# Last stage of a three-stage kernel: PE's probability transposes move to the front of each step

## What is computed

```python
def _L0_ffn_ref(x, W_gate, W_qkv):           # x = layernorm(h), 16 heads of 32
    gating = softmax(x @ W_gate.T)
    indicator = one_hot(argmax(gating)); gating_top1 = indicator * max(gating)
    q, k, v = split(x @ W_qkv.T)
    k_shared = einsum('bth,bthd->btd', indicator, k)
    v_shared = einsum('bth,bthd->btd', gating_top1, v)
    att = einsum('bhqd,bkd->bhqk', q, k_shared) / sqrt(hd)
    att = softmax(where(causal, att, -inf))
    y = einsum('bhqk,bkd->bhqd', att, v_shared)
h = h + y
```

## Time and profile before

| | us |
|---|---|
| median of 3 runs | 1482.92 |
| lowest, highest | 1481.59, 1484.98 |
| the profiled execution | 1483.9 |
| its span, first to last instruction | 1482.1 |
| PE busy in the span | 1322.8 (89%) |
| DVE, ACT, POOL busy | 816.1, 595.5, 452.5 |

### The profile page before, as it was taken

The page is one execution under the profiler, slowest core; times in us unless marked ns, Lnnn a source line. Parts: engine busy times, 40 slices in busy tenths (PEclk is TensorE's granted clock), DMA queues, the critical chain, the costliest instruction groups (busy, mean ns, idle before and its releaser), DMA issues. The chain is left out here.

```text
span 1482.1 us, 23784 instructions
## 1 busy us (share of the span) xinstructions
PE 1322.8 (89%) x8504; PEld 1109.5 (75%) x8504; DVE 816.1 (55%) x1629; ACT 595.5 (40%) x1777; POOL 452.5 (31%) x696
## 2 busy tenths in 40 slices
PE   0799999999999995599999998489899998999997
PEld 0678888888888884478888886368788787878775
DVE  8656656655566321455555552345666656566566
ACT  3443333333334221333333321234546556454646
POOL 3555445544554310233333231021221203122121
PEclk9999999999999997799999999599999999999999
DMA  3222222222222225856655411354141423514040
GB/s 147 98 87 93 93 105 88 93 93 100 86 93 93 93 90 177 241 164 171 171 162 162 147 43 44 141 107 93 37 100 36 93 70 62 116 40 101 16 93 30
DMA packets 59525, 150.71 MB, mean 102 GB/s; under 512 B 7696, under 2 KB 24336, under 8 KB 57872
## 3 DMA queue, kind: packets, MB, share of 16 engines
q1 hardware_dynamic: 59408, 149.18, 34.0%
HBM read 67.37 MB, written 56.62 MB: 84 GB/s over the span
## 5 line engine op out<-in xcount | busy, mean ns | idle before, releaser
L724 PE MATMUL psum<-wr_high,x_high 128*128 128x512 f32 x576 | 234.1, 406 | 5.0 <-DVE x_low L541 5.0
L724 PE MATMUL psum<-wr_high,x_low 128*128 128x512 f32 x576 | 228.9, 397 | 0.0
L724 PE MATMUL psum<-wr_low,x_high 128*128 128x512 f32 x576 | 228.3, 396 | 0.0
L1466 ACT ACTIVATE probs<-psum,row_max 128x256 f32<-128x256 f32 (+1 forms) x384 | 165.1, 453 | 107.6 <-issue 75.2
L1716 POOL TENSOR_TENSOR picked_rows<-picked_rows 128x768 f32<-128x768 f32 (+1 forms) x64 | 61.0, 953 | 269.6 <-DVE picked_rows L1600 265.8
L724 PEld LDWEIGHTS psum<-wr_high,x_high 128*128 128x128 f32 x576 | 109.0, 189 | 28.6 <-DVE x_low L541 5.8
L724 PEld LDWEIGHTS psum<-wr_high,x_low 128*128 128x128 f32 x576 | 108.7, 189 | 25.9
L1618 DVE TENSOR_REDUCE row_max<-psum 128x2 f32<-128x512 f32 (+1 forms) x160 | 109.5, 684 | 31.8 <-PE psum L1821 31.8
L724 PEld LDWEIGHTS psum<-wr_low,x_high 128*128 128x128 f32 x576 | 109.1, 189 | 23.4
L937 ACT ACTIVATE square_scratch<-psum 128x128 f32<-128x128 f32 x192 | 50.7, 274 | 185.4 <-PE psum L1130 185.4
L698 PE MATMUL psum<-m,basis 128*128 128x64 f32 x384 | 76.8, 283 | 40.8 <-POOL m L650 40.8
(11 more groups left out here) (200 smaller groups left out, 3027.5 us busy)
## 6 DMA issues: line engine op xcount, KB each, us to landing
qk<-stage SPq DMA_DIRECT2D x24, 512.0 KB, 2.6
v<-stage SPq DMA_DIRECT2D x24, 512.0 KB, 2.6
g<-gate_rows SPq DMA_DIRECT2D x24, 512.0 KB, 2.6
q_stack_t<-q_t_high SPq DMA_DIRECT2D x64, 192.0 KB, 4.2
q_stack_t<-q_t_low SPq DMA_DIRECT2D x64, 192.0 KB, 5.8
qk_rows<-qk SPq DMA_DIRECT2D x16, 512.0 KB, 5.5
v_rows<-v SPq DMA_DIRECT2D x16, 512.0 KB, 6.9
gate_rows_q<-g SPq DMA_DIRECT2D x16, 512.0 KB, 8.9
```

What stands on the lines that cost most here:

```text
L724: last = nc.tensor.matmul(psum[:, PB[(6 * u[1] + n) % 4], :], x[:, q, k], ww[:, w, k, :], start=c == 0, stop=c == 3 * KC - 1)
L1466: last = nc.scalar.activation(pr[:, g % 2, c], psum[:, SB[g % 3], c], ACT.Exp, scale=SCALE_F, bias=mx[:, g % 3, 1, x:x + 1], accum_out=dsu ...
```

## The change

The four probability transposes of step g are issued before the scores of step g+2 and before the side piece, instead of behind both. Nothing else differs.

```diff
--- before.py
+++ after.py
@@ -1919,10 +1919,10 @@
 
             def step(i, n, back, ahead):
                 g = NS_F * i + n
+                p_transposes(g)
                 if g + 2 < LAST:
                     scores(g + 2)
                 side(i, n, back, ahead)
-                p_transposes(g)
                 if n == 0 and back:
                     values(i - 1, 11)
                 if n in (1, 2, 3, 4):
```

## The result

| | before | after |
|---|---|---|
| median (runs) | 1482.92 (5) | 1501.17 (5) |
| lowest, highest | 1476.81, 1484.98 | 1500.75, 1502.93 |
| span of the profiled execution | 1482.1 | 1499.0 |
| ratio after/before, 95% interval | | 1.0126 [1.0103, 1.015] |

The change costs 18 us, 1.3%. The sign was forecast, the size wasn't: +7.8 us and a range up to 1499.

The account below looks back on a forecast made before the run. PE itself was taken as the bound in middle pairs, losing only a handful of stalls. About +0.7 us per pair, +4.9 for seven, made +7.8 with the last pair: 1491.7 profiled, 1490.7 median, range 1484 to 1499.

Parts of the forecast that it names:

- the two orders of waits: Middle pairs: PE newly waits near 1 us for ACT's probs before transposes 20 and 22, 0.4 to 0.7 for probs_t.
- the last pair's loop: Last pair: two steps through DVE's row maximum and copy take 3.33 us, not 2.89, with transposes now inside.
- T(20): Transposes of step 20, middle pairs: start 4.41 us after step 17's side product in both orders, set by the exponentials.
- Steps 12 to 17: Middle pairs: value products wait longer for DVE's copy at n = 16, less one gap: +0.75 us per pair.
- Middle pairs: Each pair before the last: 0.1 - 0.2 + 0.75, about +0.7 us; +4.9 for seven pairs.
- Steps 18 to 5: Stretch across two pairs, to the q product of step 6: +0.1 us, bounds -0.6 and +0.6.
- Steps 6 to 11: Middle pairs: side products cover everything and three gaps before values go: -0.2 us, bounds -0.3 and +0.3.
- The first fall: PE's drop to half clock after two stalls, 1192 to 1194 in the fourth pair: no longer certain, no price given.
- the second one: PE's drop to half clock after the logits, 1198 to 1200 in the fourth pair: stays as it was.
- My sign of being wrong: Over a middle pair: PEclk moving away from 0.95 by more than 0.02 would show the forecast wrong.
- My first rival: Clock still falls in step 2 or anew around step 0, slowing work ahead of logits: +6.3 us, 1497; chance 0.16.
- Last pair: Pair without side pieces: four intervals at 0.44 us plus a start later by about 1.1: +2.9 us, bounds +1.8 and +3.7.

Follow-up runs that it names:

- the changed kernel with the filling products: The changed kernel plus 10 products of 512 columns per pair, results unread, where PE only waits: 1492.81 us, ratio 1.007.
- the kernel before with filling products: The kernel before plus seven products of 512 columns per pair, results unread, where PE waits: 1479.85 us, ratio 0.9988.

## Why the prediction was wrong

The forecast for the profile was +7.8 us and +16.9 were measured. Of the 9.1 missed, 5.6 lie in the six middle pairs, 2.3 in the last pair and 0.8 behind it, and 0.4 ahead of the first step.

**Right.** The sign; the two orders of waits; the last pair's loop, forecast 3.33 and measured 3.36; T(20) at +4.41, T(22) at 9.89 for 9.8; values at n = 14 at +8.97 in both kernels. Steps 12 to 17 are nearly right, forecast +0.75 and measured +0.86. Of it 0.85 lie between values at n = 14 and the end of the side product of step 17: up to the k transposes 4.72 us became 5.20, and from there 4.70 became 5.07.

**Middle pairs, forecast +0.7 each, measured +1.6.** The step that failed most is "Steps 18 to 5", then "Steps 6 to 11". To see it the clock has to be taken out, and the windows from the end of step 17's side product to the q product of step 6 allow that. The first two lines are of the kernel before and of the changed one, each with 6.8 us at half clock on work, the third of the changed kernel with the filling products, which had none, and the fourth, also without, of the kernel with the new order in steps 18 to 5 only:

```profile
1244.63:1270.69 26.06, 22.84 (x193) 0.87 0.12 42
```

```profile
1184.93:1211.81 26.88, 23.18 (x193) 0.87 0.12 41
```

```profile
1116.12:1139.90 23.78, 22.55 (x202) 1.00 0.12 45
```

```profile
1184.93:1207.88 22.95, 19.91 (x193) 1.00 0.14 47
```

By the first two the new order takes 0.8 us more at the same clock, where I had +0.1. The logits start at +14.08 where it is +13.55 in a pair that has no half clock ahead of them: +0.5, forecast +0.2. Then I had the first q product 0.4 earlier, since T(23) and T(24) would be out of the way. Only T(23) is: between logits and q product the old order has T(23), values, scores, and the new one has values, T(24), scores. At full clock the q product starts at +18.13 where it was about +17.6 (an estimate, from +17.79 in the kernel before with filling products, less 0.15 for 0.3 us at half clock): +0.5. The last 0.3 us come up to the q product of step 6, with T(26) waiting for its exponentials as forecast. The fourth line shows what these 0.8 us hang on: with T(26) still behind that q product the part takes 22.95 us, 0.8 less, late logits and all. At the front of the part one T has gone and nothing is gained, since PE waits there; at its end one T has come in.

In steps 6 to 11 (first q product of step 6 to the end of the side product of step 11) 21.12 us went to 21.24, where I had -0.2. The gap of 0.09 between T and values is no longer there, but T behind values takes 0.49 up to the scores, not 0.44, and the values start about 0.1 late behind a side product. The gap goes with the values wherever they stand. I had taken the lower bound, zero.

So at equal clock the order costs +0.8, +0.1 and +0.9, in all 1.8 us a pair, where I had 0.7.

**Clock.** It did not make the changed kernel slower as against before: three of its six middle pairs have one stretch of half clock in place of two. What it cost on average is 2.3 us a pair, against 2.5 before (what the pairs take above the same windows at full clock), so it gives 0.2 back. The step is off all the same. The first fall did go, as I thought possible, and was worth 0.3 us only. But I had the second one stay as it was. In the fourth pair, which I walked, it was 3.4 us long before and is 6.8 now, on the end of the logits, values, T(24), scores and the first q product. That q product takes 3.75 us, at full clock 2.17, and T(24) and the scores behind it 0.90 and 0.86 where 0.49 and 0.46 are usual. My sign of being wrong, PEclk moving by more than 0.02, is met too (0.974 for 0.948 in three pairs). My first rival looked for a cost ahead of the logits; it came behind them.

**Last pair, forecast +2.9, measured +5.2.** Loop right, count wrong. I let four of the six intervals between values from n = 6 to n = 18 take the extra time; all six took 0.40 to 0.48 us, 2.8 in all. The interval with `normalise` and y_rows loses time as well, for it is the same loop through DVE with `normalise` in it, and T of step 13 now stands between values and scores there too. And values at n = 6 came 2.4 us late, counted from the k transposes, not 1.1 (1.9 in the run with the new order in the last pair alone); 2.2 of it are there at n = 4. PE in steps 4 to 6, and DVE:

```profile
1463.65 0.42 PE L1850 MATMUL psum<-probs_t,v_shared 128*32 128x128 f32 x8 [0.72 <-DVE probs_t L1628]
...
1465.91 0.66 PE L1832 MATMUL psum<-ident,probs 128*128 128x128 f32 x4 [0.19 <-ACT probs L1466]
...
1467.69 0.64 PE L1850 MATMUL psum<-probs_t,v_shared 128*32 128x128 f32 x16 [0.68 <-ACT probs_t L1475]
```

```profile
1466.26 0.69 DVE L1637 TENSOR_TENSOR y_normed<-psum,den 128x512 f32<-128x512 f32 x1
1466.86 0.68 DVE L1628 COPY probs_t<-psum 128x512 f32<-128x512 f32 x1
```

The values at n = 4 (1463.65) wait 0.72 us for DVE's copy of step 3, which I had not looked at; T(26) waits for the exponentials as forecast; the values at n = 6 (1467.69) start 0.83 behind DVE's copy of step 5 (1466.86), which stands behind `normalise`. ACT's copy, which the profile names, is of step 6, and these values don't read it.

**Start and end.** The first pair, one of the seven at +0.7, took 0.6 us more, and 0.4 us came ahead of its first step, where nothing was changed. After the last T, where I had 0, it is +0.8, and that is the clock: PEclk is 0.59 over this end, and the last values and y_rows take 1.03 and 1.11 us where they took 0.64 and 0.66. With the new order in the last pair alone PEclk is 0.87 there and the same end takes 8.47 us. So this part isn't the price of the order.

**The bound of the measurement.** I wrote that 0.2% can be told from no change. The kernel before alone spreads over 1473 to 1491 us in 30 runs, and its profiled execution, with 0.95 in every middle pair, is from the upper half.

**What stays open.** Which pairs fall to half clock, and when, follows neither from the idle time filled nor from the size of the products next to it. No run settled it. Nor did one separate transposes from other work in their effect on the clock. The rule that I had set beside rival 1, of the Trainium skill, page "TensorE: Matmul & The Clock Gate", section "Part 4: PE-mode transpose", is neither borne out nor refuted.

## What to carry to other kernels

If an engine's pieces are reordered, find for each new wait the queue that its releaser stands in: here T moved up, but the copy that empties its bank stayed behind row_max and picks, and only moving both (and leaving the stretch without side pieces alone) gave a gain, 0.5%. Each alone was a loss of 1.3 and 1.7%. And a walk and the measured stretch that it is set against must have the same time at half clock in them, or both none. When pieces are moved, write out what stands between two fixed points in both orders: one piece gone from there is no gain if another has come in.

## What the hardware showed that I had not expected

A stretch of 3.4 us at half clock costs a fixed sum where PE works on: 62.2, 63.8 and 65.3 us for a pair with PEclk 1.00, 0.97 and 0.95, whichever of two kernels, about 1.6 us each. Where PE would have waited anyway it costs about 0.3: in the kernel before two pairs with the same 0.95 last 64.36 and 65.55 us. And large products mixed in among the small ones did not keep the clock up by themselves: PEclk of a pair fell as far as 0.92 (0.90 in the changed kernel).
